# Gathering some of the source one-hots of an edge count from an identity table in DRAM

## The reference

```python
N, R = 1250, 34                      # nodes, relations
# attention layers: softmax over the edges that enter a node
e = leaky_relu(s_src[src] + s_dst[dst]); ee = exp(e - segment_max(e, dst)[dst])
out = segment_sum(ee / denom[dst] * h[src], dst)
# relational layer
cnt = segment_sum(1, type * N + dst); mean = segment_sum(x[src], type * N + dst) / max(cnt, 1)
h1 = einsum('rni,rio->no', mean, W_rel) + x @ W_root
# GCN
deg = segment_sum(1, dst) + 1; out = segment_sum(xw[src] * dinv[src] * dinv[dst], dst)
```

## Time and profile before

| | |
|---|---|
| median of 3 runs | 3329.17 us (3328.10 to 3329.29) |
| the profiled execution | 3328.76 us, its span 3327.0 us |
| TensorE, VectorE busy | 3134.6, 2302.0 us |
| ScalarE, GpSimd busy | 1487.3, 1669.9 us |
| counting stage | about 217 to 453 us |

### The profile page before, as it was taken

How to read it: one execution, slowest core, us unless ns; L and a number is a source line. 1 busy time by engine, 2 the same in 40 slices (tenths; PEclk the granted TensorE clock), 3 DMA queues, 4 the chain that set the end, 5 groups by cost and what they waited for, 6 DMA issues and landing times.

```text
span 3327.0 us, 60088 instructions
## 1 busy us (share of the span) xinstructions
PE 3134.6 (94%) x17307; PEld 1954.5 (59%) x17307; DVE 2302.0 (69%) x4665; ACT 1487.3 (45%) x2713; POOL 1669.9 (50%) x1374
## 2 busy tenths in 40 slices
PE   6989989997899999999999999999999999879998
PEld 4444457986556666666666666666666665434545
DVE  8989997959865555555546878788787865443335
ACT  3757766747443343433434565554655532110010
POOL 3730000001666666666524666566565636777763
PEclk9989999999899999999999999999999999999999
DMA  3020012011333333433334556565565534665542
GB/s 95 2 77 0 0 43 97 1 52 54 136 116 124 130 102 127 133 105 130 110 131 162 179 168 201 166 197 175 173 205 169 182 134 144 189 213 158 157 142 75
DMA packets 228627, 411.92 MB, mean 124 GB/s; under 512 B 37765, under 2 KB 177924, under 8 KB 228535
## 3 DMA queue, kind: packets, MB, share of 16 engines
q1 hardware_dynamic: 167664, 268.22, 23.2%
q0 software_dynamic: 60480, 142.01, 15.1%
q10 hardware_dynamic: 390, 0.50, 0.1%
HBM read 259.19 MB, written 151.32 MB: 123 GB/s over the span
## 4 chain that ended last, share of the span: by engine, by line
PE 73%; DVE 10%; issue 5%; DMA 5%; POOL 5%; ACT 2%; DVEq 1%; ACTq 0%; POOLq 0%
PE bank L2455 18%; PE bank L2457 18%; PE bank L2458 18%; PE bank L2444 4%; DMA arena<-y_half,idx_now 4%; POOL placed_dram L781 3%; DVE arena L1651 3%; PE bank L2297 2%; PE bank L2432 2%; PE bank L2431 2%; PE bank L2357 2%; DVE arena L1708 2%; PE bank L2702 2%; DVE arena L1746 2%; DVE arena L1650 1%
## 5 line engine op out<-in xcount | busy, mean ns | idle before, releaser
L2455 PE MATMUL bank<-arena 128*128 128x384 f16 x3675 | 1199.7, 326 | 1.2 <-ACT arena L1254 1.2
L2457 PE MATMUL bank<-arena 128*128 128x384 f16 x3675 | 1198.6, 326 | 0.0
L2458 PE MATMUL bank<-arena 128*128 128x384 f16 x3675 | 1198.6, 326 | 0.0
L1254 ACT ACTIVATE arena<-bank,winv 128x384 f32<-128x384 f32 x700 | 400.4, 579 | 835.9 <-PE bank L2458 834.5
L1901 DVE SCALAR_TENSOR_TENSOR arena<-bank,winv,arena 128x384 f32<-128x384 f32 x525 | 318.7, 615 | 379.3 <-PE bank L2458 375.8
L2455 PEld LDWEIGHTS bank<-arena 128*128 128x128 f16 x3675 | 359.9, 98 | 247.5 <-issue 14.9
L2458 PEld LDWEIGHTS bank<-arena 128*128 128x128 f16 x3675 | 359.8, 98 | 237.7 <-issue 0.5
L2457 PEld LDWEIGHTS bank<-arena 128*128 128x128 f16 x3675 | 360.2, 98 | 233.1 <-issue 5.1
L1825 DVE SCALAR_TENSOR_TENSOR arena<-arena,wscale 128x1152 f16<-128x1152 f32 x245 | 379.9, 1586 | 162.5 <-ACT arena L1187 153.5
L851 POOL DMA_INDIRECT arena<-y_half,idx_now x360 | 399.0, 1108 | 162.5 <-issue 99.6
L865 POOL DMA_INDIRECT arena<-y_half,idx_now x360 | 354.1, 984 | 116.8 <-issue 97.0
(11 more groups left out here) (274 smaller groups left out, 4508.2 us busy)
## 6 DMA issues: line engine op xcount, KB each, us to landing
y_half<-arena SPq DMA_DIRECT2D x306, 384.0 KB
arena<-in_L_gnn_W_rel_dram SPq DMA_DIRECT2D x68, 1152.0 KB, 8.0
arena<-y_half,idx_now POOLq DMA_INDIRECT x720, 3.1
y_half<-arena SPq DMA_DIRECT2D x34, 294.0 KB
cT_dram<-arena SPq DMA_DIRECT2D x1, 5625.0 KB
arena<-cT_dram SPq DMA_DIRECT2D x9, 625.0 KB, 4.5
arena<-in_x_dram SPq DMA_DIRECT2D x10, 384.0 KB, 8.7
xu_dram<-arena SPq DMA_DIRECT2D x9, 384.0 KB, 2.6
```

What stands on the lines that cost most here:

```text
L1254: nc.scalar.activation(y[half][:, :, c * CQ:(c + 1) * CQ], acc, ACT.Copy, scale=scale).then_inc(r_copied, 1)
L2455: nc.tensor.matmul(acc, h, w_hi[m - 1][:, k, :], start=fresh and k == 0, stop=False, skip_group_check=True)
L2457: nc.tensor.matmul(acc, h, w_lo[m - 1][:, k, :], start=False, stop=False, skip_group_check=True)
L2458: ins = nc.tensor.matmul(acc, l, w_hi[m - 1][:, k, :], start=False, stop=k == KH - 1, skip_group_check=True)
```

## The change

The loops over the stage now run over turns of TURN = 6 units. In even units of a turn the wide one-hots of tiles 2 and 3, in odd units that of tile 3, are no longer made by VectorE: three of eight. GpSimd gathers them instead by an indirect DMA each, one row of an identity matrix in DRAM for each edge, by the edge's source (`eye_rows`, 135 gathers of 128 rows of 2500 bytes in all). The rows go to nine buffers, one for each such tile of a turn; before a buffer is written again GpSimd waits until TensorE is through with the unit six before. The matrix `eye_dram` is written at the start of the kernel: GpSimd clears a band `eye` in SBUF, ScalarE copies the identity into it, and SP stores ten row blocks of it by eleven DMAs, shifted views of the one band. VectorE converts the source numbers of the tiles to integers (`idx_eye`) before the sorted edges are announced. The 34 relation columns of a gathered tile are still in `oh_s`, so TensorE's last bank (226 source and 34 relation columns) takes two matmuls in such a tile. ScalarE makes no one-hots; VectorE makes all four narrow ones, with those of the gathered tiles ahead of its last wide one. The first six units' gathers stand before GpSimd's additions to `Wux`, the others behind them. Later users of the semaphores that the gathers borrow count `EYES_READ` more.

```diff
@@ -43,6 +43,7 @@
...
+    TURN, EYES = 6, 2
...
@@ -143,6 +144,7 @@
...
+        eye_dram = nc.dram_tensor("eye_dram", (NT * P, N // 2), F32, kind="Internal").ap()
...
@@ -173,7 +175,12 @@
...
-        assert scatV + SCAT * 12 + ET * 8 <= B0
+        eyeV = scatV + SCAT * 12 + ET * 8
+        EYE_AT = (NT - 2) * P
+        eye = view(eyeV, [(EYE_AT + N) // 2])
+        eye_f = eye.bitcast(F16)
+        assert N % 4 == 2 and eyeV + (EYE_AT + N) * 2 <= B0
+        idx_eye = row_a[:, 0:UNITS * EYES].bitcast(I32).rearrange("p (u t) -> p u t", t=EYES)
...
@@ -204,8 +211,15 @@
...
-        last_d = [view(XU + CB * UT * P * 2 + i * P * 2, [P], F16) for i in range(CB)]
-        assert UNITS % CB == 0
+        assert UNITS % TURN == 0 and TURN % CB == 0
+
+        def by_eye(j):
+
+            return range(UT - 1 - (j % 2 == 0), UT)
+
+        EYE_SLOT = {p: n for n, p in enumerate((j, t) for j in range(TURN) for t in by_eye(j))}
+        oh_eye = [view(M0 + n * N * 2, [N // 2]) for n in range(len(EYE_SLOT))]
+        assert len(EYE_SLOT) * N * 2 <= NT * N * 2
...
@@ -404,6 +418,8 @@
...
+        eye_made = sem("eye_made")
+        eye_loaded = g_loaded[0:TURN]
...
@@ -533,6 +549,7 @@
...
+        EYES_READ = [len(by_eye(k)) * (UNITS // TURN) if k < TURN else 0 for k in range(4 * UT)]
...
@@ -551,7 +568,7 @@
...
-            return k, (g_loaded + tail_loaded)[k], i * (m // units) + (c // units + before + 1)
+            return k, (g_loaded + tail_loaded)[k], i * (m // units) + (c // units + before + 1 + EYES_READ[k])
...
@@ -585,6 +602,15 @@
...
                 .then_inc(rel_inv_stored, 16)
+            sp.wait_ge(eye_made, 2)
+            for n in range(NT - 1):
+                at = (EYE_AT - n * P) // 2
+                sp.dma_start(eye_dram[n * P:(n + 1) * P, :], eye[:, at:at + N // 2]).then_inc(eye_made, 16)
+            zero, at = (N - P) // 2, (EYE_AT + P) // 2
+            last = eye_dram[(NT - 1) * P:NT * P, :]
+            sp.dma_start(last[:, 0:zero], eye[:, at:at + zero]).then_inc(eye_made, 16)
+            at = (EYE_AT - (NT - 1) * P) // 2 + zero
+            sp.dma_start(last[:, zero:N // 2], eye[:, at:at + P // 2]).then_inc(eye_made, 16)
             sp.wait_ge(edges_placed, 16 * SCAT)
...
@@ -771,6 +797,7 @@
...
+            nc.gpsimd.memset(eye_f[:, 0:EYE_AT + N], 0.0).then_inc(eye_made, 1)
...
@@ -782,10 +809,29 @@
...
 
+            def eye_rows(us):
+
+                for u in us:
+                    if u >= TURN:
+                        pool.wait_ge(cnt_psum, (u - TURN + CB) * len(CBANKS) + len(CBANKS))
+                        pool.nop(nofuse=True)
+                    j = u % TURN
+                    for t in by_eye(j):
+                        nc.gpsimd.indirect_dma_start(
+                            out=oh_eye[EYE_SLOT[j, t]], out_offset=None, in_=eye_dram,
+                            in_offset=bass.IndirectOffsetOnAxis(ap=idx_eye[:, u, t - UT + EYES:t - UT + EYES + 1], axis=0))\
+                            .then_inc(eye_loaded[j], 16)
+
+            pool.wait_ge(eye_made, 16 * (NT + 1) + 2)
+            pool.wait_ge(h_ready, NT * HALVES)
+            pool.wait_ge(sorted_ready, 1)
+            pool.nop(nofuse=True)
+            eye_rows(range(TURN))
             pool.wait_ge(wu_loaded, 16)
...
                 nc.gpsimd.tensor_tensor(at, at, ident[:, :], ALU.add).then_inc(wux_ready, 1)
+            eye_rows(range(TURN, UNITS))
 
...
@@ -965,6 +1011,8 @@
...
             nc.scalar.activation(credit[:, 0:1], epsc[:, 0:1], ACT.Sqrt)
+            act.wait_ge(eye_made, 1)
+            nc.scalar.copy(eye_f[:, EYE_AT:EYE_AT + P], ident[:, :]).then_inc(eye_made, 1)
             for g, (a, b) in enumerate(X_GROUPS):
...
@@ -1012,33 +1060,17 @@
...
             nc.scalar.copy(credit[:, 0:1], ones[:, 0:1]).then_inc(cnt_copied, len(CBANKS))
-            def count_copy(i, c):
-                b = act.value_load(unit_bucket[0:1, bass.ds(i * CB + c, 1)], min_val=0, max_val=NT - 1)
+            def count_copy(u):
+                b = act.value_load(unit_bucket[0:1, bass.ds(u, 1)], min_val=0, max_val=NT - 1)
                 for j, (lo, hi) in enumerate(CBANKS):
-                    act.wait_ge(cnt_psum, i * (CB * len(CBANKS)) + ((c + CB) * len(CBANKS) + j + 1))
+                    act.wait_ge(cnt_psum, u * len(CBANKS) + (CB * len(CBANKS) + j + 1))
                     nc.scalar.copy(countsf[:, bass.ds(b * CW + lo, hi - lo)],
...
 
-            def last_onehot(u, s):
-
-                v = last_d[s % CB]
-                if s >= CB:
-                    act.wait_ge(cnt_psum, u * len(CBANKS) + len(CBANKS))
-                nc.scalar.activation(v, iota[:, 0:P], ACT.Abs, bias=dst_s[:, bass.ds(u * UT + (UT - 1), 1)],
-                                     scale=-1.0).then_inc(cnt_abs, 1)
-                act.wait_ge(cnt_abs, u + 1)
-                nc.scalar.activation(oh_d[:, s % CB * UT + UT - 1, :], v, ACT.Relu, bias=ones[:, 0:1],
-                                     scale=-1.0).then_inc(cnt_act, 1)
-
             act.wait_ge(sorted_ready, 1)
-            for c in range(CB):
-                last_onehot(c, c)
-            with act.Fori(0, UNITS // CB - 1) as i:
-                for c in range(CB):
-                    count_copy(i, c)
-                    last_onehot(i * CB + (c + CB), c + CB)
-            for c in range(CB):
-                count_copy(UNITS // CB - 1, c)
+            with act.Fori(0, UNITS // TURN) as i:
+                for j in range(TURN):
+                    count_copy(i * TURN + j)
 
...
@@ -1224,7 +1256,7 @@
...
-                    act.wait_ge(g_loaded[place * UT + t], (uses + 1) * 16)
+                    act.wait_ge(g_loaded[place * UT + t], (uses + (1 + EYES_READ[place * UT + t])) * 16)
...
@@ -1625,6 +1657,8 @@
...
             after(nc.vector.tensor_scalar(src_s[:, :], src_s[:, :], float(HALF), None, ALU.add))
+            nc.vector.tensor_copy(idx_eye[:, :, :],
+                                  src_s[:, :].rearrange("p (u t) -> p u t", t=UT)[:, :, UT - EYES:UT])
             nc.vector.scalar_tensor_tensor(typ_s[:, :], typ_s[:, :], float(TLOW), whole, ALU.mult, ALU.add)\
...
@@ -1635,21 +1669,22 @@
...
 
-            with dve.Fori(0, UNITS // CB) as i:
-                for j in range(CB):
-                    u = i * CB + j
+            with dve.Fori(0, UNITS // TURN) as i:
+                for j in range(TURN):
+                    u, f = i * TURN + j, j % CB
                     dve.wait_ge(cnt_psum, u * len(CBANKS) + len(CBANKS))
-                    nc.vector.tensor_tensor(oh_s[:, j * UT:(j + 1) * UT, N:CW],
+                    nc.vector.tensor_tensor(oh_s[:, f * UT:(f + 1) * UT, N:CW],
                                             iota[:, 0:R].unsqueeze(1).broadcast_to([P, UT, R]),
...
                                             ALU.is_equal)
-                    for t in range(UT):
-                        at = bass.ds(u * UT + t, 1)
-                        s = j * UT + t
-                        if t < UT - 1:
-                            nc.vector.tensor_scalar(oh_d[:, s, :], iota[:, 0:P], dst_s[:, at], None, ALU.is_equal)
-                        nc.vector.tensor_scalar(oh_s[:, s, 0:N], iota[:, 0:N], src_s[:, at], None,
-                                                ALU.is_equal).then_inc(cnt_oh, 1)
+                    here = [t for t in range(UT) if t not in by_eye(j)]
+                    dsts = list(range(UT))
+                    for t in here:
+                        for d in [t] if t != here[-1] else dsts[dsts.index(t):]:
+                            nc.vector.tensor_scalar(oh_d[:, f * UT + d, :], iota[:, 0:P], dst_s[:, bass.ds(u * UT + d, 1)],
+                                                    None, ALU.is_equal)
+                        nc.vector.tensor_scalar(oh_s[:, f * UT + t, 0:N], iota[:, 0:N], src_s[:, bass.ds(u * UT + t, 1)],
+                                                None, ALU.is_equal).then_inc(cnt_oh, 1)
 
...
@@ -2230,19 +2265,30 @@
...
             ins.then_inc(cnt_psum, CB * len(CBANKS))
-            with pe.Fori(0, UNITS // CB) as i:
-                for jj in range(CB):
-                    u = i * CB + jj
+            MADE_AT = [sum(UT - len(by_eye(k)) for k in range(j)) for j in range(TURN + 1)]
+            MADE = MADE_AT[TURN]
+            with pe.Fori(0, UNITS // TURN) as i:
+                for jj in range(TURN):
+                    u = i * TURN + jj
                     for j, (lo, hi) in enumerate(CBANKS):
...
                         for t in range(UT):
+                            s = jj % CB * UT + t
                             if j == 0:
-                                pe.wait_ge(cnt_oh, u * UT + t + 1)
-                                if t == UT - 1:
-                                    pe.wait_ge(cnt_act, u + 1)
-                            ins = nc.tensor.matmul(bank[j][:, 0:hi - lo], oh_d[:, jj * UT + t, :],
-                                                   oh_s[:, jj * UT + t, lo:hi],
```

(16 more changed lines are left out.)

## The result

The changed kernel takes 3301.03 us (median of 4 runs, 3299.16 to 3303.02), the kernel before 3329.23 beside it: ratio 0.9918 [0.9902, 0.9933]. Forecast was 3319 (3303 to 3341): 10 us faster were expected, 28 us came, just under the range. The profiled execution of the changed kernel is 3300.49 us long, its span 3298.8.

A forecast was written before the change was run, and what follows sets the result against it. VectorE was taken to bound the counting stage, before and after. 45 pairs x (5.16 - 4.90) = 11.7 us saved, 1.5 and 0.3 lost, so 10 saved: 3319 us, range 3303 to 3341.

The forecast's parts named there:

- Step (1): Counting stage, VectorE: three of eight wide one-hots go, two narrow ones come; 4.07 us a pair against 5.16.
- Step (2): Counting stage, TensorE: splitting the last bank in three gathered tiles adds 0.04 to 0.34 us a pair; 4.5 taken.
- Step (3): Counting stage, ScalarE: loses 180 one-hot instructions, some 75 us of work no one waited for; worth nothing by itself.
- Step (4): Counting stage, GpSimd's gathers: 1.42 us each, holding VectorE up 0.26 each, 0.78 a pair; VectorE then 4.85.
- TensorE binds: Rival, counting stage: hold-up hidden or small, TensorE's 4.5 us a pair decides; 3304, at best 3292; chance 0.12.
- The clean row: Last stage's gathers beside fp32 one-hots, issued every 1.25 us; cited for TensorE binds as showing no mutual delay.
- Step (5): Counting stage, GpSimd's other costs: additions to Wux 3.6 us, about four pauses 8.4; 204 us in all against VectorE's 220.
- Step (6): Start of the counting stage: first gathers hardly late, up to 3 us lost once, 1.5 counted; index cast 0.3 at most.
- Steps (7) and (8): DMA engines 0.7 busy in counting, landing 0.4 us longer than 3.1; writing the identity table at kernel start costs nothing.
- GpSimd binds: Rival, the slower side: gather cost decides over VectorE from 1.54 us; 3320 at 1.58, 3338 at 1.71; chance 0.25.
- GpSimd starves: Rival: each gather waits for a whole wide one-hot at two points, 2.16 us; some 3395; chance 0.10.
- Nothing: Rival: narrow work and hold-ups of 0.35 us a gather refill VectorE to 5.1 a pair; 3326 to 3331; chance 0.08.

The follow-up runs named there:

- the run with added columns: Changed kernel with two instead of three of eight wide one-hots gathered, plus a 512-column matmul of zeros per unit: 3314.7 beside 3326.56, single runs.
- idle gathers: Changed kernel with VectorE making all eight wide one-hots, the 135 gathers still issued but their rows unread: 3416.89 us, single run.
- one more narrow one-hot: Changed kernel with one more unused narrow one-hot a unit on VectorE: 3305.96 us, ratio 0.9936, beside 3302.23 for the changed kernel.
- sessions of 3400: Sessions where the kernel before takes 3400 to 3410 us instead of 3329; the unedited changed kernel has ratio 1.0001 in one.
- 3407: Session named by the kernel before's time, in which the unedited changed kernel was run again: ratio 1.0001 [0.9992, 1.0011].
- sessions of 3329: Sessions where the kernel before takes about 3329 us; the unedited changed kernel has ratio 0.9918 in one.
- two of eight: Changed kernel with two of eight wide one-hots gathered instead of three: ratio 0.9909 in one session, 0.9913 beside the changed kernel's 1.0001 in another.

## Why the prediction was wrong, point by point

- Step (1), VectorE's own work: 4.07 forecast, 4.10 measured. Right.
- Step (2), TensorE: 4.5 forecast. Changed kernel 4.44; a 34-column matmul costs 0.03. Right within its bounds, too high by 0.06, and in part by luck: the three splits cost 0.09 where the step took 0.22, and a hand-over that it did not count makes up for some of it. Of the 4.44, 4.36 are TensorE's own by the run with added columns (for two split tiles; a third adds 0.03); about 0.05 are the hand-over with VectorE, a remainder and not measured by itself.
- Step (3): ScalarE's one-hots were worth nothing. Right as far as the trace tells: its copies wait for TensorE (87.7 of 89.3 us of the idle time before those of 512 columns). It was not tried alone.
- **Step (4) failed.** I took 0.26 us of VectorE's time for each gather from the sort's scatters, because it was the only stage with the same VectorE work, and weighed "another engine's work is the same" above "the transfer is another". The hold-up is 0.00 over 128 partitions, for gathers and scatters alike, 0.20 over 125, and 0.00 over 112. Why 125 partitions hold VectorE up is open. It was the term that made VectorE the bound: 45 x 0.78 = 35 us of VectorE time that were not there. My lower bound was 0, so the rival "TensorE binds" carried about the right outcome at 3304, with a chance of 0.12; the range began at 3303, above its best cases, and missed 3301. The gather's issue itself was well sized: 1.42 forecast, 1.39 measured with idle gathers (0.96 to 1.20 and 0.30 between them), 1.33 with one more narrow one-hot.
- The clean row had 128 partitions and the scatter row 125; the row of the one-hots beside the scatter says 125x128. I compared what ran beside the transfers and not their shapes.
- Step (5), the additions: their length was forecast as 3.6 and is 2.50, but their price was put on GpSimd alone. They stop VectorE. Of the four pauses of 2.1 us the trace shows two (2.02 before 242.05, 2.05 before 384.59), and the pairs beside the second stay at 4.44.
- Step (6), the start: 1.5 forecast, 4.6 lost. The first wait (2.58) is that for the first eye rows beside the load of Wux, the DMA engines at 0.87; I had called it "hardly late". With that load held back it was 1.15.
- Steps (7) and (8): DMA share 0.76 for 0.7; a gather lands 4.3 us after its issue (median) where 3.5 were forecast; the table cost nothing (the last scatter is issued 1.0 us earlier than before, at 202.1).
- Rivals: "GpSimd binds", the slower side with a chance of 0.25, did not come in the first trace, but in the sessions of 3400 something near it did: not by the price of a gather (1.25 to 1.45), but by signals that come late beside them. The time is then that of before. "GpSimd starves" did not come. "Nothing" came in those sessions, by another road than the one given.
- Two small sums: with the pair of 4.90 the gathers decide over VectorE from 1.56 a gather, not from 1.54; and 61 us above the 3338 of the slower side are 3399, not 3395. Neither moves the forecast.

## What to carry to other kernels

When a price is borrowed from another stage, compare the transfer's shape (partitions above all) before the company it has; a single run with the operation left idle, its result unused, gives the price by itself. Where three engines end within 8% of each other, take the variant that leaves GpSimd a pause between its indirect DMAs: two gathers of eight kept the whole gain in the sessions where three lost it, at a stage no longer than three had at their best. And time a change in more than one session before its gain is believed, if it adds indirect DMAs in a row.

## What the runs showed of the hardware that was not expected

- An indirect DMA over 125 partitions: GpSimd record at least 1.19 to 1.21 us and VectorE's fp16 one-hots held up by 0.20 each (0.26 in the sort); over 128 (record from 0.95) and 112 (from 0.97) nothing. Over 128 it is the same for a gather of 2500 bytes a row and a scatter of 8, over 125 for gather and scatter of 8.
- In sessions of 3400, beside indirect DMAs over 128 partitions one behind another, releases between the other engines come late: mostly by 0.7 to 2 us beside the counts' gathers (1.3 to 1.8 us apart), and by up to 30 us in the sort at a pitch of 1.27, after some 18 scatters. They are prompt again once GpSimd has paused (1.9 us between groups of six; some 10 us after the last scatter of a row of 90). At 125 partitions and 1.58 us a scatter, 90 in a row, nothing of it (longest wait of VectorE for TensorE in the sort 0.8 at 3407). What is late, and where, the trace does not tell; the same gathers without a pause show nothing of it in the sessions of 3329, and whether the sort's scatters over 128 partitions would show it in a session of 3329 was not tried. What makes a session one or the other is unknown; one chip had first the one (3329) and half an hour later the other (3410).
- The last stage of the kernel issues gathers over 128 partitions in a row too, and in the changed kernel in the session of 3407 waits of up to 17 us stand there, where the first trace's longest of the same waits are 7.9 and 3.1:

```profile
ACT idx_now L1267 <- issue: 42.7, 6, 17.3
...
ACT arena L1459 <- remote: 38.8, 3, 14.9
```

```profile
ACT arena L1459 <- PE bank L2739: 26.4, 9, 3.1
```

(Columns: who waited for what, us in total, times, longest; the first two lines at 3407, the last from the first trace.) Two traces show where such a session's time goes: the last stage's first gather starts at 2735.15 in the changed kernel's first trace and at 2735.02 in that of two of eight at 3407, and the spans are 3298.8 and 3376.0. All 77 us lie behind that gather. The granted clock is lower there too (0.88 from 2700 to 3050 us, for 0.96), which can be a cause or come of TensorE's waits. That the kernel before loses its 70 to 80 us in the same place is argued from this, not shown: there is no trace of before from such a session.
- Six tensor_tensor of 128x128 fp32 on GpSimd (2.5 to 2.8 us) stop VectorE's fp16 one-hots for their whole length, at the start of the stage and at its end alike.
